# Storing turned pairs in 512-byte runs and loading each back in one transfer of 4 KB runs

## Chip, cores and metric

The kernel runs on one core of one Trainium2 chip. The metric is device time in microseconds, the median over runs of one execution each. Engines are named as in the profile: PE (TensorE), DVE (VectorE), ACT (ScalarE), POOL (GpSimd) and SP (SyncE, which issues every transfer of this kernel on one queue).

## What is computed

A gated layer over `x` of 64 sequences x 128 tokens x 512 features, float32: a cross-attention branch whose score matrix is summed over the batch, and a feed-forward branch, each added to `x` through a tanh gate.

```python
# attention branch on LN(x), context c
Q, K, V = LN(x) @ Wh, c @ Wh, c @ Wh          # per head, 4 heads of 128
A = max(|sum_b(Q K^T / sqrt(hd)) * decay|, 1)
O = A V
Y = (O - mean(O)) / sqrt(var(O) + 1e-3) * gamma + beta
x1 = x + tanh(g1) * ((relu(LN(x) @ Wg) * Y) @ Wo)
# feed-forward branch
x2 = LN(x1)
out = x1 + tanh(g2) * (silu(x2 @ Gate * gs) * (x2 @ Up * us)) @ Down * ds
```

## The kernel before

The 64 sequences are 64 tiles `t` of 128 tokens. The kernel runs in three stages. The first (to about 345 us) makes V, W and the score sum group by group of four sequences. The second, `first_groups`, runs 8 groups of 15 steps: 11 steps multiply 512 tokens of x2 with the gate and up weights (`up_mm`), 4 steps multiply the hidden tiles with the down weights (`down_mm`). Between these steps, the attention branch of pairs of tiles `q` is carried on in 13 pieces, a new pair every 3.5 steps (`pieces`, `first_step`). The third stage takes the other 32 tiles in 4 passes of 8, with products of sums and differences of weights (`seven`, `down_of`).

TensorE wants Y and x2 turned, features on the partitions, and in float32 split into a high and a low part. From the third pair on it doesn't turn them itself. The path is:

- DVE transposes each tile of 128 tokens x 512 features in blocks of 32 x 32 (`y_blocks` into `tbuf`, L1006; `x2_blocks` into `xbuf`, L1053). This turns inside each group of 32 partitions.
- SyncE stores the pair to DRAM (`y_out`, L377, to `wy_scratch`; `x2_out`, L381, to `x2_scratch`), 4 KB from each partition.
- SyncE loads it back with the blocks where they belong: `blocks_in` (L421 to L426) issues four transfers, one for each 32 partitions of the destination, in runs of 128 bytes. `y_in` fills `turned[0]`, `x2_in` fills `turned[1]` for the second stage, and `pair_in` fills `fa` and `fb` for the third.
- ACT applies gamma and beta to Y (`y_pair_affine`, L666) in place, DVE multiplies with W (`wy_pair_mul`, L1017), ACT and POOL split the product (`wy_pair_hi`, L706; `wy_pair_lo`), and PE multiplies it with Wo (`wo_pair`). For x2, ACT copies the high part (`x2_pair_hi`, L711) and DVE makes the low one (`x2_pair_lo`, L1057); in the third stage `operand_hi` (L729), `operand_lo` and `combine` prepare seven operands from `fa` and `fb`.

Every engine runs its own list in program order, and waits on semaphores at its head. So what sets the order around the change is: on SyncE, in pair `q`'s pieces, `y_out` (piece 3), `y_in` (4; it waits for the store and for the multiply of the pair before), `w_load` (5), `x_again` (6), `x2_out` and `x1_store` (12), and `x2_in` at steps 9 and 12 of a group; on ACT, `x2_pair_hi` at steps 11 and 13, ahead of that step's pieces; on DVE, `x2_pair_lo` in the same steps, ahead of the transposes, the multiply and x1 of these steps, and ahead of the next `finish` (L1167), which frees the bank that PE's next product needs.

Of the kernel before, what the change touches and what calls it, by code (L numbers as in the profile page):

```python
# [9 lines left out]
NS = 8  # L10
# [65 lines left out]
def gated_layer(nc, x, ctx_t, wh, wh_t, wg, wo, gate_t, up_t, down_t, cols, rows, decay, eye, out):  # L76
# [6 lines left out]
    with stack:  # L83
# [26 lines left out]
        stg = misc[:, 512:1216]  # L110
        tbuf = misc[:, 0:1024].rearrange("p (t n) -> p t n", t=2)
# [4 lines left out]
        xbuf = placed("xbuf", [128, 2, 512])  # L116
        a_parts = [a[:, :].rearrange("p (h n) -> p h n", h=4) for a in a_sb]
# [54 lines left out]
        oper = [[over(f"op{i}{part}", *units[2 * i + part], [128, 2, 512], f32r) for part in range(2)] for i in range(7)]  # L172
        fa = over("fa", "reg", 44, [128, 2, 4, 256])
        fb = over("fb", "reg", 60, [128, 2, 4, 256])
        hall = over("hall", "reg", 0, [128, NI, 1024])
# [47 lines left out]
        bank_p6 = pz  # L223

        def before_split(o):

            a1, a2, b1, b2 = fa[:, :, 0:2, :], fa[:, :, 2:4, :], fb[:, :, 0:2, :], fb[:, :, 2:4, :]
            return {A1: a1, T1: a1, A2: a2, T4: a2, T3: b1, B2: b2, T2: b2}[o]

        def split(o, i):  # L230

            return oper[o][i][:, :, :].rearrange("p k (h n) -> p h k n", h=2)

# [37 lines left out]
        def wt_of(q):  # L271

            return xbuf[:, :, :].rearrange("p t (k n) -> p (t k) n", n=256) if q == 1 else raw[:, 2:4, :].rearrange("p t (k n) -> p (t k) n", n=256)

# [15 lines left out]
        def _(e):  # L290
# [81 lines left out]
            def y_out(q):  # L372

                p.wait_ge("wyb", 2 * q - 2)
                if q > 2:
                    p.wait_ge("wyl", 64 * (q - 2))
                e.dma_start(wy_s.rearrange("t p n -> p t n"), tbuf).then_inc(s["wys"], 16)  # L377
# [33 lines left out]
            def pair_in(q):  # L411

                p.wait_ge("x2s", 16 * (q - 1))
# [5 lines left out]
                blocks_in(x2_s[q], to[:, q % 2, :, :], "x2l")  # L419

            def blocks_in(scratch, dst, name):  # L421

                src = scratch.rearrange("t (u r) (c a j) -> a r c (t u) j", u=4, c=4, a=4)
                for a in range(4):
                    to = dst[32 * a:32 * a + 32, :, :].rearrange("r c (x j) -> r c x j", j=32)
                    e.dma_start(to, src[a]).then_inc(s[name], 16)  # L426

            def y_in(q):
                p.wait_ge("wys", 16 * (q - 1))
                p.wait_ge(*(("wm", q + 2) if q > 2 else ("wm", 4)))  # L430
                blocks_in(wy_s, turned[0], "wyl")

            def x2_in(q):
                p.wait_ge("x2s", 16 * (q - 1))
                if q > 2:
                    p.wait_ge("tb2e", q + 2)
                blocks_in(x2_s[q], turned[1], "x2l")

# [162 lines left out]
        def _(e):  # L601
# [61 lines left out]
            def affine(dst, src):  # L663

                for k in range(4):
                    last = e.activation(dst[:, k, :], src[:, k, :], ACT.Identity, bias=colsb[:, 2 * NI + 6 + k:2 * NI + 7 + k],  # L666
                                        scale=colsb[:, 2 * NI + 2 + k:2 * NI + 3 + k])
                last.then_inc(s["aff"])
# [8 lines left out]
            def y_pair_affine(q):  # L677
                p.wait_ge("wyl", 64 * (q - 1))
                affine(turned[0], turned[0])

# [27 lines left out]
            def x2_pair_hi(q):  # L708
                p.wait_ge("x2l", 64 * (q - 1))
                p.wait_ge("um", 11 * (q // 2))  # L710
                e.copy(x2_pair(q, 0), turned[1][:, :, :]).then_inc(s["tb2h"])  # L711

# [6 lines left out]
            def operand_hi(m, k):  # L719
                o = (A1, B2, A2, T1, T2, T3, T4)[k]  # L720
                if k == 0 and m == 0:
                    p.wait_ge("um", NI * NS)
                elif k == 0:
                    p.wait_ge("p4", NI * m)
                if k == 0:
                    p.wait_ge("x2l", 64 * (2 * NS + 4 * m + 2))
# [30 lines left out]
            def split_hi(m, part):  # L757
# [5 lines left out]
                else:  # L763
                    p.wait_ge("wo", B)
                    p.wait_ge("wylo", B // 2 - 2)
                    p.wait_ge("tb2e", 2 + 2 * NS)
                    p.wait_ge("x2s", 16 * (B // 2 - 2))
                e.copy(hsp[t % 2][0][:, i0:i1, :], hall[:, i0:i1, 128 * i:128 * i + 128]).then_inc(s["hsh"])  # L768
# [144 lines left out]
        def _(e):  # L913
# [85 lines left out]
            def y_blocks(t):  # L999
                p.wait_ge("nr", t + 1)  # L1000
                if t >= 6:
                    p.wait_ge("wys", 16 * (t // 2 - 2))
                else:
                    p.wait_ge("alo", 1)
                    p.wait_ge("wolo", 4)
                e.transpose(tbuf[:, t % 2, :], nbuf[:, t % 2, :]).then_inc(s["wyb"])  # L1006

# [41 lines left out]
            def x2_blocks(t):  # L1049
                p.wait_ge("xn2", t + 1)  # L1050
                if t >= 6:
                    p.wait_ge("x2s", 16 * (t // 2 - 2))
                e.transpose(xbuf[:, t % 2, :], xn[:, t % 2, :]).then_inc(s["x2b"])  # L1053

            def x2_pair_lo(q):
                p.wait_ge("tb2h", q + 3)
                e.tensor_tensor(x2_pair(q, 1), turned[1][:, :, :], f(x2_pair(q, 0)), ALU.subtract).then_inc(s["tb2e"])  # L1057

            def combine(m, k):

                a1, a2, b1, b2 = fa[:, :, 0:2, :], fa[:, :, 2:4, :], fb[:, :, 0:2, :], fb[:, :, 2:4, :]
                dst, x, y = ((a1, b1, a1), (b1, b2, b1), (b2, b2, a1), (a2, a2, b2))[k]
# [3 lines left out]
                p.wait_ge("opt", 4 * m + k)  # L1066
                p.wait_ge("x2l", 64 * (2 * NS + 4 * m + 2))
                e.tensor_tensor(dst, x, y, ALU.subtract).then_inc(s["opt"])
# [862 lines left out]
```

## Time and profile before

| | |
|---|---|
| median of 3 runs | 1529.16 us (1528.46 to 1529.73) |
| the profiled execution | 1533.71 us |
| its span, first to last instruction | 1531.7 us |
| mean granted TensorE clock | 0.996 |
| busy PE, DVE, ACT, POOL | 98%, 69%, 45%, 47% |
| DMA packets | 374598, of which 258336 under 512 B |

In the profile a line such as L1017 is the line of kernel.py that issued the instruction. `out<-in` names the tiles, "SPq" is an issue on SyncE's queue, and a wait or idle time is followed by what ended it. A chain is the work that ended last, followed back step by step. "PEclk" is the TensorE clock that was granted as a share of full speed. The DMA share is the mean busy share of the core's 16 DMA engines.

### The profile page before, as it was taken

The page shows a single profiled execution, that of the slowest core. Times are in us where ns is not written, and L with a number is a line of the kernel's source. Part 1 is how long each engine was busy: PE and PEld are TensorE (multiplying, and loading weights), DVE is VectorE, ACT ScalarE, POOL GpSimd, SP SyncE. Part 2 cuts the span into 40 slices and gives each one's busy share as a digit, 9 for nine tenths or more (in the row PEclk, how much of TensorE's full clock was granted, in tenths as well). Part 3 has the DMA queues.
Part 4 walks back from the last instruction along what each step waited for, and adds up shares of the span by engine and source line. Part 5 has one row for each costly group of instructions (what it writes and reads, how often), then busy time and mean ns, then how long its engine had stood idle before and what let it go on. Part 6 is the DMA issues. An engine that isn't in the chain of part 4 may idle for free.

```text
span 1531.7 us, 20329 instructions
## 1 busy us (share of the span) xinstructions
PE 1500.3 (98%) x7226; PEld 1259.3 (82%) x7226; DVE 1058.3 (69%) x1497; ACT 684.0 (45%) x1067; POOL 723.4 (47%) x775
## 2 busy tenths in 40 slices
PE   6999999999899999999999999999999999999998
PEld 5888888887788888888887888888788888888887
DVE  6677778785557676577765777563767777778772
ACT  3444434445454545455353554534344444343442
POOL 4556666762353544445352544524227338237236
PEclk9999999999999999999999999999999999999999
DMA  6888888866678687787776777686273473472422
GB/s 227 270 266 267 262 281 286 265 216 205 199 220 219 200 213 222 210 252 221 220 228 181 211 219 216 182 239 170 89 214 127 114 213 104 142 209 94 132 102 83
DMA packets 374598, 305.93 MB, mean 200 GB/s; under 512 B 258336, under 2 KB 284320, under 8 KB 374304
## 3 DMA queue, kind: packets, MB, share of 16 engines
q1 hardware_dynamic: 374496, 304.61, 66.6%
q8 instruction: 59, 0.97, 0.2%
q14 instruction: 43, 0.35, 0.1%
HBM read 200.23 MB, written 117.31 MB: 207 GB/s over the span
## 4 chain that ended last, share of the span: by engine, by line
PE 83%; DVE 5%; DMA 4%; POOL 3%; ACT 2%; issue 2%; SPq 2%; DVEq 0%; ACTq 0%; POOLq 0%
PE ps L1670 37%; PE pyb L1554 8%; PE po L1670 8%; PE ptb L1670 5%; PE pyb L1670 5%; PE ps L1589 5%; PE po L1554 4%; PE pyb L1654 3%; PE ptb L1654 3%; PE ptb L1658 2%; PE pyb L1658 2%; SPq L426 1%; PE ptb L1559 1%; DMA wy_scratch<-misc 1%; POOL reg L1432 1%
## 5 line engine op out<-in xcount | busy, mean ns | idle before, releaser
L1385 POOL TENSOR_SCALAR rs<-mv 128x1 f32<-128x1 f32 (+1 forms) x132 | 53.1, 402 | 296.7 <-DVE mv L1034 141.3
L1670 PE MATMUL ps<-reg,gate 128*128 128x512 f32 x704 | 177.6, 395 | 4.4 <-DVE tmp L1167 2.6
L1473 POOL TENSOR_TENSOR reg<-tmp,reg 128x512 fp32r<-128x512 f32 x88 | 118.0, 1342 | 131.2 <-ACT reg L717 131.2
L1554 PE MATMUL pyb<-reg,xreg 128*128 128x512 f32 x720 | 178.6, 396 | 0.8 <-DVE xreg L947 0.8
L1670 PE MATMUL ps<-reg,up 128*128 128x512 f32 x704 | 174.4, 390 | 0.0
L1670 PE MATMUL ps<-op,wbuf 128*128 128x512 f32 x704 | 173.9, 389 | 0.0
L1670 PE MATMUL ps<-xreg,reg 128*128 128x512 f32 x704 | 163.4, 390 | 1.3 <-DVE tmp L1167 1.3
L1457 POOL TENSOR_TENSOR p5b<-p5b,p1b 128x512 f32<-128x512 f32 x44 | 57.0, 1295 | 218.1 <-ACT p5b L741 218.1
L1670 PEld LDWEIGHTS ps<-reg,gate 128*128 128x128 f32 x704 | 132.2, 190 | 31.9 <-issue 3.0
L1670 PEld LDWEIGHTS ps<-reg,up 128*128 128x128 f32 x704 | 132.8, 189 | 27.8
L1670 PEld LDWEIGHTS ps<-xreg,reg 128*128 128x128 f32 x704 | 131.5, 188 | 29.1 <-DVE tmp L1167 1.8
L1670 PEld LDWEIGHTS ps<-op,wbuf 128*128 128x128 f32 x704 | 132.1, 188 | 27.4
L1554 PEld LDWEIGHTS pyb<-reg,xreg 128*128 128x128 f32 x720 | 131.8, 188 | 27.6 <-DVE xreg L947 1.5
L1468 POOL TENSOR_TENSOR hsp<-hall,hsp 128x640 fp32r<-128x640 f32 (+2 forms) x72 | 136.6, 1914 | 34.6 <-ACT hsp L768 33.5
L1670 PE MATMUL po<-op,wbuf 128*128 128x512 f32 x528 | 134.6, 389 | 0.0
L1160 DVE SCALAR_TENSOR_TENSOR tmp<-ps,colsb,tmp 128x512 f32<-128x512 f32 x88 | 65.5, 744 | 87.5 <-PE ps L1670 83.3
L1436 POOL TENSOR_TENSOR wyt<-raw,wyt 128x1024 fp32r<-128x1024 f32 x30 | 75.1, 2504 | 90.8 <-ACT wyt L706 90.8
L1670 PEld LDWEIGHTS po<-op,wbuf 128*128 128x128 f32 x528 | 99.1, 188 | 20.6
L778 ACT ACTIVATE tmp<-ps,colsb 128x512 f32<-128x512 f32 x88 | 60.6, 688 | 121.3 <-PE ps L1670 108.7
L1589 PE MATMUL ps<-reg 128*128 128x256 f32 x768 | 101.1, 284 | 1.5 <-DVE misc L953 1.1
L1589 PEld LDWEIGHTS ps<-reg 128*128 128x128 f32 x768 | 96.9, 191 | 5.4 <-ACT tmp L626 1.5
L1388 POOL TENSOR_TENSOR rs<-rs,nhalf 128x1 f32<-128x1 f32 (+1 forms) x132 | 88.8, 672 | 11.0
(153 smaller groups left out, 2829.5 us busy)
## 6 DMA issues: line engine op xcount, KB each, us to landing
wbuf<-ws_scratch SPq DMA_DIRECT2D x44, 896.0 KB, 4.9
xr<-in_x SPq DMA_DIRECT2D x63, 512.0 KB, 5.7
raw<-in_ctx_t SPq DMA_DIRECT2D x32, 512.0 KB, 4.7
w_scratch<-tmp SPq DMA_DIRECT2D x64, 256.0 KB, 5.0
v_scratch<-tmp SPq DMA_DIRECT2D x64, 256.0 KB, 4.2
raw<-v_scratch SPq DMA_DIRECT2D x32, 512.0 KB, 6.1
x_scratch<-xr SPq DMA_DIRECT2D x32, 512.0 KB, 4.6
xr<-x_scratch SPq DMA_DIRECT2D x32, 512.0 KB, 6.0
```

Source lines behind the costliest of these rows:

```text
L778: e.activation(tmp[:, m % 3, :], banks[2 * (n % 2)], ACT.Silu, scale=colsb[:, j:j + 1]).then_inc(s["si"])
L1160: e.scalar_tensor_tensor(tmp[:, m % 3, :], banks[2 * (n % 2) + 1], colsb[:, NI + j:NI + j + 1], tmp[:, m % 3, :], ALU.mult, ALU.mult).then ...
L1388: e.tensor_tensor(dst, dst, nhalf[:, 0:dst.shape[-1]], ALU.pow).then_inc(s[name])
L1436: e.tensor_tensor(wyt[1][:, :, :], wt_of(q), f(wyt[0][:, :, :]), ALU.subtract).then_inc(s["wylo"])
L1457: e.tensor_tensor(p5b[n % 2][:, :], p5b[n % 2][:, :], p1b[n % 2][:, :], ALU.add).then_inc(s["p15"])
L1468: e.tensor_tensor(hsp[t % 2][1][:, i0:i1, :], hall[:, i0:i1, 128 * i:128 * i + 128], f(hsp[t % 2][0][:, i0:i1, :]), ALU.subtract).then_inc ...
L1473: e.tensor_tensor(hid[1][:, m % 11, :], tmp[:, m % 3, :], f(hid[0][:, m % 11, :]), ALU.subtract).then_inc(s["hlo"])
L1554: last = e.matmul(dst, lhs[a], rhs[b], start=(k == 0 and i == 0), stop=(k == n - 1 and i == 2))
L1589: last = e.matmul(ps[t % 2][:, h, :, :], ct[g % 2][i][:, h, 128 * b:128 * b + 128], wh_and_z(q, h, b), start=(n == 0), stop=(n == 2))
L1654: e.matmul(py(t), wyt_of(t)[0][:, k, :], wos[i][k], start=(k == 0 and i == 0), stop=False)
L1658: last = e.matmul(py(t), wyt_of(t)[1][:, k, :], wos[0][k], start=False, stop=(k == 3))
L1670: last = e.matmul(dst, l, r, start=(k == 0 and i == 0), stop=(k == n - 1 and i == 1), skip_group_check=sums)
```

## The change

The two scratch tensors get the shape [j 32, (a t) 8, u 4, 128], so that what one destination partition needs lies together in 4 KB. DVE's transposes write their blocks in another order (`blocks_to`, `blocks_of`), so that each partition holds eight runs of 128 elements (512 bytes). A pair is stored in four transfers, one for each 32 partitions `u`, in runs of 512 bytes (`blocks_out`). It is loaded in one transfer to 128 partitions, 4 KB each, whose source is walked as 4 `a`, 32 `j`, 4 KB. The tokens and features now lie in each loaded partition as 8 groups (32 tokens each) of 4 runs (feature blocks) of 32 elements, and the instructions that read it (L666, L711, L1017, L1057, `operand_hi`, `operand_lo`, `combine`) walk it in these runs (`by_part`, `tokens_by_32`, `half_of`). The number of compute instructions and their element counts stay. A load counts 16 on its semaphore instead of 64, a store 64 instead of 16.

```diff
-        wy_s = nc.dram_tensor("wy_scratch", [2, 128, D], f32, kind="Internal").ap()
-        x2_s = nc.dram_tensor("x2_scratch", [B // 2, 2, 128, D], f32, kind="Internal").ap()
+        wy_s = nc.dram_tensor("wy_scratch", [32, 8, 4, 128], f32, kind="Internal").ap()
+        x2_s = nc.dram_tensor("x2_scratch", [B // 2, 32, 8, 4, 128], f32, kind="Internal").ap()
...
+        def half_of(pairs, i):
+
+            return pairs[:, :, :].rearrange("p q (x d n) -> p (q x) d n", x=8, d=2)[:, :, i, :]
...
+        def by_part(pair):
+
+            return pair.rearrange("p (x c r) -> p c x r", x=8, c=4)
+
+        def tokens_by_32(pair):
+            return pair.rearrange("p c (x r) -> p c x r", x=8)
+
+        def blocks_to(pair, t):
+
+            return pair.rearrange("p (a t c r) -> p t a c r", a=4, t=2, c=4)[:, t % 2, :, :, :]
+
+        def blocks_of(tile):
+
+            return tile.rearrange("p (c a j) -> p a c j", c=4, a=4)
...
             def x2_out(q):
                 p.wait_ge("x2b", 2 * q - 2)
-                e.dma_start(x2_s[q].rearrange("t p n -> p t n"), xbuf[:, :, :]).then_inc(s["x2s"], 16)
+                blocks_out(x2_s[q], xbuf[:, :], "x2s")
...
+            def blocks_out(scratch, pair, name):
+
+                for u in range(4):
+                    e.dma_start(scratch[:, :, u, :], pair[32 * u:32 * u + 32, :].rearrange("j (x n) -> j x n", x=8)).then_inc(s[name], 16)
...
             def blocks_in(scratch, dst, name):
 
-                src = scratch.rearrange("t (u r) (c a j) -> a r c (t u) j", u=4, c=4, a=4)
-                for a in range(4):
-                    to = dst[32 * a:32 * a + 32, :, :].rearrange("r c (x j) -> r c x j", j=32)
-                    e.dma_start(to, src[a]).then_inc(s[name], 16)
+                e.dma_start(dst, scratch.rearrange("j (a t) u n -> a j (t u n)", a=4)).then_inc(s[name], 16)
...
-                e.tensor_tensor(wt_of(q), wt_of(q), turned[0][:, :, :], ALU.mult).then_inc(s["wm"])
+                wt = tokens_by_32(wt_of(q))
+                e.tensor_tensor(wt, wt, by_part(flat(turned[0])), ALU.mult).then_inc(s["wm"])
...
-                e.transpose(xbuf[:, t % 2, :], xn[:, t % 2, :]).then_inc(s["x2b"])
+                e.transpose(blocks_to(xbuf[:, :], t), blocks_of(xn[:, t % 2, :])).then_inc(s["x2b"])
```

## Rows read from the trace of the kernel before

**Rows 1.** The page: span, and part 1 (busy us, share, instructions).

```profile
span 1531.7 us, 20329 instructions
...
PE 1500.3 (98%) x7226; PEld 1259.3 (82%) x7226; DVE 1058.3 (69%) x1497; ACT 684.0 (45%) x1067; POOL 723.4 (47%) x775
```

**Rows 2.** TensorE's waits, 380 to 1110 us: total, times, longest us.

```profile
PE ps L1670 <- DVE tmp L1167: 3.9, 2, 2.6
...
PE pyb L1654 <- ACT wyt L706: 1.0, 1, 1.0
...
PE ps L1670 <- DVE tmp L1160: 0.4, 1, 0.4
```

**Rows 3.** Windows: length, busy PE, PEld, DVE, ACT, POOL, clock, DMA share, GB/s.

```profile
406.00:408.00 2.00, 2.00 (x10) 1.68 (x9) 0.00 (x0) 1.65 (x3) 1.19 (x2) 1.00 1.06 411
...
552.72:635.17 82.45, 82.45 (x388) 69.19 (x387) 56.55 (x83) 43.81 (x66) 38.99 (x47) 1.00 0.79 217
...
840.00:850.00 10.00, 9.04 (x33) 7.31 (x34) 9.59 (x15) 4.76 (x7) 7.31 (x9) 0.83 0.36 110
...
1044.00:1046.00 2.00, 2.00 (x10) 1.65 (x10) 0.33 (x1) 1.88 (x3) 0.82 (x1) 1.00 1.08 172
```

**Rows 4.** SyncE's queue, timelines 396:480 and 800:845: start, us.

```profile
437.19 3.55 SPq L426 DMA_DIRECT2D turned<-wy_scratch  x4
...
817.71 4.06 SPq L426 DMA_DIRECT2D turned<-wy_scratch  x4
...
821.81 0.67 SPq L381 DMA_DIRECT2D x_scratch<-xbuf  x1
...
823.98 6.55 SPq L426 DMA_DIRECT2D turned<-x_scratch  x4
```

**Rows 5.** Chain that ended last, 795 to 860 us: start, us.

```profile
821.81 3.37 DMA x_scratch<-xbuf
...
833.55 1.06 ACT reg L711
```

**Rows 6.** Chain that ended last, 390 to 480 us.

```profile
443.97 6.18 DMA x_scratch<-xr
...
458.70 1.06 ACT reg L711
```

**Rows 7.** Lines L426, L381: issue in ns, least, median, most.

```profile
L426 SPq DMA_DIRECT2D turned<-wy_scratch x120: 557/668/3211, 411.8 to 1008.5; - x120
...
L381 SPq DMA_DIRECT2D x_scratch<-xbuf x30: 360/665/1113, 443.6 to 1052.8; - x30
```

**Rows 8.** The page's part 6: KB each, median us to landing.

```profile
out<-xr SPq DMA_DIRECT2D x31, 512.0 KB, 2.8
```

**Rows 9.** Timelines of DVE, ACT and PE at two chains' ends.

```profile
478.17 1.23 DVE L1057 TENSOR_TENSOR reg<-turned,reg 128x1024 fp32r<-128x1024 f32 x1 [1.18 <-ACT reg L711]
...
481.49 2.00 PE L1670 MATMUL ps<-reg,gate 128*128 128x512 f32 x8
...
923.57 1.05 ACT L711 CAST reg<-turned 128x1024 fp32r<-128x1024 f32 x1 [6.09 <-DMA turned<-x_scratch]
...
927.04 1.05 ACT L706 CAST wyt<-raw 128x1024 fp32r<-128x1024 f32 x1 [2.42 <-DVE raw L1017]
...
930.41 1.98 PE L1654 MATMUL pyb<-reg,wyt 128*128 128x512 f32 x8
```

**Rows 10.** Lines L1006, L1017, L666: duration in ns, least, median, most.

```profile
L1006 DVE STREAM_TRANSPOSE misc<-nbuf x60: 659/711/714, 398.6 to 999.2; 128x512 f32<-128x512 f32 x60
...
L1017 DVE TENSOR_TENSOR raw<-raw,turned x30: 1179/1226/2298, 421.2 to 1028.6; 128x1024 f32<-128x1024 f32 x30
...
L666 ACT ACTIVATE turned<-turned,colsb x120: 586/588/604, 418.2 to 1025.9; 128x256 f32<-128x256 f32 x120
```

**Rows 11.** ScalarE's waits, whole span: total, times, longest us.

```profile
ACT reg L711 <- DMA turned<-x_scratch: 45.8, 9, 8.2
```

**Rows 12.** Timeline of ScalarE, 1055 to 1096 us.

```profile
1068.74 1.05 ACT L729 CAST op<-fa 128x1024 fp32r<-128x1024 f32 x1
```

More of the change, by code:

```diff
@@ L110, in gated_layer @@
         stg = misc[:, 512:1216]
-        tbuf = misc[:, 0:1024].rearrange("p (t n) -> p t n", t=2)
+        tbuf = misc[:, 0:1024]
         wyt = [placed(f"wyt{i}", [128, 4, 256], f32r) for i in range(2)]
@@ L115, in gated_layer @@
         a_sb = [placed(f"a{i}", [128, 512], f32r) for i in range(2)]
-        xbuf = placed("xbuf", [128, 2, 512])
+        xbuf = placed("xbuf", [128, 1024])
         a_parts = [a[:, :].rearrange("p (h n) -> p h n", h=4) for a in a_sb]
@@ L172, in gated_layer @@
         oper = [[over(f"op{i}{part}", *units[2 * i + part], [128, 2, 512], f32r) for part in range(2)] for i in range(7)]
-        fa = over("fa", "reg", 44, [128, 2, 4, 256])
-        fb = over("fb", "reg", 60, [128, 2, 4, 256])
+        fa = over("fa", "reg", 44, [128, 2, 1024])
+        fb = over("fb", "reg", 60, [128, 2, 1024])
         hall = over("hall", "reg", 0, [128, NI, 1024])
@@ L223, in gated_layer, with flat @@
         bank_p6 = pz
+        def half_of(pairs, i):
+            return pairs[:, :, :].rearrange("p q (x d n) -> p (q x) d n", x=8, d=2)[:, :, i, :]
         def before_split(o):
-            a1, a2, b1, b2 = fa[:, :, 0:2, :], fa[:, :, 2:4, :], fb[:, :, 0:2, :], fb[:, :, 2:4, :]
-            return {A1: a1, T1: a1, A2: a2, T4: a2, T3: b1, B2: b2, T2: b2}[o]
+            a1, a2, b1, b2 = half_of(fa, 0), half_of(fa, 1), half_of(fb, 0), half_of(fb, 1)
+            return {A1: a1, T1: a1, A2: a2, T4: a2, T3: b1, B2: b2, T2: b2}[o].rearrange("p x (k r) -> p x k r", k=2)
         def split(o, i):
-            return oper[o][i][:, :, :].rearrange("p k (h n) -> p h k n", h=2)
+            return oper[o][i][:, :, :].rearrange("p k (x r) -> p x k r", x=16)
+        def flat(pair):
+            return pair[:, :, :].rearrange("p c n -> p (c n)")
+        def by_part(pair):
[6 more added lines that the diff above has]
+            return tile.rearrange("p (c a j) -> p a c j", c=4, a=4)
         def down_bank(t):
@@ L271, in wt_of @@
         def wt_of(q):
-            return xbuf[:, :, :].rearrange("p t (k n) -> p (t k) n", n=256) if q == 1 else raw[:, 2:4, :].rearrange("p t (k n) -> p (t k) n", n=256)
+            return xbuf[:, :].rearrange("p (k n) -> p k n", k=4) if q == 1 else raw[:, 2:4, :].rearrange("p t (k n) -> p (t k) n", n=256)
         def tile_of(pair, t):
@@ L375, in y_out @@
                 if q > 2:
-                    p.wait_ge("wyl", 64 * (q - 2))
-                e.dma_start(wy_s.rearrange("t p n -> p t n"), tbuf).then_inc(s["wys"], 16)
+                    p.wait_ge("wyl", 16 * (q - 2))
+                blocks_out(wy_s, tbuf, "wys")
             def x2_out(q):
                 p.wait_ge("x2b", 2 * q - 2)
-                e.dma_start(x2_s[q].rearrange("t p n -> p t n"), xbuf[:, :, :]).then_inc(s["x2s"], 16)
+                blocks_out(x2_s[q], xbuf[:, :], "x2s")
             def sums_store(u):
@@ L411, in pair_in @@
             def pair_in(q):
-                p.wait_ge("x2s", 16 * (q - 1))
+                p.wait_ge("x2s", 64 * (q - 1))
                 if q < 2 * NS + 4:
@@ L665, in affine @@
                 for k in range(4):
-                    last = e.activation(dst[:, k, :], src[:, k, :], ACT.Identity, bias=colsb[:, 2 * NI + 6 + k:2 * NI + 7 + k],
+                    last = e.activation(dst[:, k], src[:, k], ACT.Identity, bias=colsb[:, 2 * NI + 6 + k:2 * NI + 7 + k],
                                         scale=colsb[:, 2 * NI + 2 + k:2 * NI + 3 + k])
@@ L677, in y_pair_affine @@
             def y_pair_affine(q):
-                p.wait_ge("wyl", 64 * (q - 1))
-                affine(turned[0], turned[0])
+                p.wait_ge("wyl", 16 * (q - 1))
+                affine(by_part(flat(turned[0])), by_part(flat(turned[0])))
             def wy_hi(t):
@@ L708, in x2_pair_hi @@
             def x2_pair_hi(q):
-                p.wait_ge("x2l", 64 * (q - 1))
+                p.wait_ge("x2l", 16 * (q - 1))
                 p.wait_ge("um", 11 * (q // 2))
-                e.copy(x2_pair(q, 0), turned[1][:, :, :]).then_inc(s["tb2h"])
+                e.copy(tokens_by_32(x2_pair(q, 0)), by_part(flat(turned[1]))).then_inc(s["tb2h"])
             def hidden_hi(m):
@@ L725, in operand_hi @@
                 if k == 0:
-                    p.wait_ge("x2l", 64 * (2 * NS + 4 * m + 2))
+                    p.wait_ge("x2l", 16 * (2 * NS + 4 * m + 2))
                 if k >= 3:
@@ L766, in split_hi @@
                     p.wait_ge("tb2e", 2 + 2 * NS)
-                    p.wait_ge("x2s", 16 * (B // 2 - 2))
+                    p.wait_ge("x2s", 64 * (B // 2 - 2))
                 e.copy(hsp[t % 2][0][:, i0:i1, :], hall[:, i0:i1, 128 * i:128 * i + 128]).then_inc(s["hsh"])
@@ L1001, in y_blocks @@
                 if t >= 6:
-                    p.wait_ge("wys", 16 * (t // 2 - 2))
+                    p.wait_ge("wys", 64 * (t // 2 - 2))
                 else:
@@ L1005, in y_blocks @@
                     p.wait_ge("wolo", 4)
-                e.transpose(tbuf[:, t % 2, :], nbuf[:, t % 2, :]).then_inc(s["wyb"])
+                e.transpose(blocks_to(tbuf, t), blocks_of(nbuf[:, t % 2, :])).then_inc(s["wyb"])
             def wy_mul(t):
@@ L1066, in combine @@
                 p.wait_ge("opt", 4 * m + k)
-                p.wait_ge("x2l", 64 * (2 * NS + 4 * m + 2))
+                p.wait_ge("x2l", 16 * (2 * NS + 4 * m + 2))
                 e.tensor_tensor(dst, x, y, ALU.subtract).then_inc(s["opt"])
```

16 lines of the change are left out of this document (8 added, 8 removed).

## The prediction

> **What bounds the kernel now.** I read the page first: TensorE (PE) is busy 1500.3 of 1531.7 us [rows 1], so a transfer can move the end only where PE stands still. Next come PE's waits: from 380 to 1110 us, where the changed code runs, it waits 3.9 us for `finish` (L1167), 1.0 us for the W*Y halves (L706) and 0.4 us for the hidden tile (L1160) [rows 2]; the waits on L1042 and L1047 there end before the first changed transfer. The windows give the price of one such stop: PE idled 2.6 us at 838 to 841 and the granted clock in 840 to 850 was then 0.83, so 1.7 us went with it; over whole groups without a stop PE is busy 82.45 of 82.45 us at clock 1.00 [rows 2, 3]. So the ceiling on any gain is 2.6 + 1.7 + 1.0 + 0.4 = 5.7 us. The 1.3 us left of the 3.9 (later) come from the operand preparation on VectorE, whose loads are long in, and I leave them.
>
> **The stop at 838 us.** The queue's timeline and the chain of waits show it: SyncE's four parts of the Y load take 4.06 us to issue, only then go out the x2 store, the x1 store and the W load; the x2 store lands 3.37 us after issue, and the four parts of the x2 load, issued from 823.98 to 830.53 us with a wait inside, land at 833.55 [rows 4, 5]. ScalarE stands in `x2_pair_hi` (L711) until then, VectorE behind it in `x2_pair_lo`, and queued behind that are two transposes, two residual adds with their statistics and the `finish` that frees PE's bank. PE is 2.6 us late. The same chain at 451 to 464 us costs 1.0 us (L711, transposes, L1017, L706) [rows 6].
>
> **What the queues can carry.** A plain load in long runs moved 411 GB/s at a DMA share near 1; loads in 128-byte runs moved 172 GB/s at the same share [rows 3]. So the 524,288 bytes of a pair take 3.1 us now, on all 16 engines, and would take 1.3 us in 4 KB runs on 16. One engine alone then carries about 411/16 = 25.7 GB/s.
>
> **Part 1, the store.** One transfer becomes four of 32 partitions. For the issue the nearest rows are L426, also 32 partitions each (median 0.67, least 0.557 us), against 0.36 to 0.67 for the single store [rows 7]: about 2.4 us for four instead of 0.5, so +1.9 us of SyncE per pair, and the last quarter leaves 1.8 us later. It applies 30 times to Y and 30 times to x2; behind it on SyncE stand the x1 store, the W load and the next x load. In data: 128-byte runs cost 3.1 us for 256 runs on each engine, 12.1 ns a run, of which 5 ns is the bytes; with the same 7 ns over, 64 runs of 512 B cost 64 x (20 + 7) = 1.7 us, against 1.3. Bounds 1.3 and 3.1; I take 1.7.
>
> **Part 2, the load.** Four issues become one: SyncE gets back 3 x 0.67 = 2.0 us at the median and up to 4.06 - 0.6 = 3.5 in the stopped chain. It pays for part 1. The data is the open point. The new source is walked as 4 blocks `a`, then 32 rows `j`, then 4 KB. Every other transfer that I find in the kernel has a first walk of 128, 32 or 352. If the hardware deals a transfer out by its first walk, this one goes to 4 engines, not 16: 131,072 B on each, 5.1 us, where the others get nothing. No row of before decides it. The Trainium skill ("DMA: Bandwidth & Descriptors", sections on why a DMA increments its semaphore by 16 and on rules for kernel authors) says just this: the number of engines is the largest up to 16 that divides the slowest dimension of both sides, so 4 here. That rule speaks against the change, and no run here shows it yet.
>
> With 4 engines, the stopped chain goes so (a fixed 1.5 us from issue to first data: the 512 KB store of the output at the median lands in 2.8 us [rows 8], less 1.3). The Y load is issued at 817.7, and fills the four until 817.7 + 1.5 + 5.1 = 824.3. The x2 quarters wait behind it and end at 826.0 (825.2 before). The x2 load is issued at 826.1; x1 store and W load are ahead of it, 1.3 us each, to 828.6; it lands at 833.7, or 0.5 to 1 us later if part of the 1.5 us comes at the end: +0.2 to +1.2 against 833.55. I take +0.9. The chain at 451: the Y load issued at 437.2 [rows 4] ends at 443.8, W load, x2 and x1 stores behind it by 448.1 to 448.6 (before, the x1 store landed at 450.15 [rows 6]), so x again and V load start 1.6 us sooner and the x2 load, 5.1 instead of 3.1 us and 0.6 less in issue, lands within 1 us of 458.70. I take 0.
>
> **Where there is slack.** In the other groups the distance from the end of the chain to the PE instruction that needs it is: `x2_pair_lo` ends at 479.40, the gate product starts at 481.49, 2.1 us; L706 ends at 928.1, PE's `wo_pair` starts at 930.41, 2.3 us [rows 9]. I found no shorter one in the rest. A shift of 0.9 is hidden there. Over a group of 82.45 us the DMA share is 0.79, 65 us, of which 6.3 pair loads of 3.1 are 19.5 [rows 3]; the four engines would then hold 45.5 + 8.6 x 0.4 + 6.3 x 5.1 = 81 us of 82.45, the others far less. Shares over 1 occur [rows 3], so these seconds overlap in part and the true load is lower. That is the danger of this change.
>
> **Part 3, engine work.** DVE's transposes, ScalarE's copies and affines and the multiplies keep their element counts and now walk runs of 32 elements. The transposes (711 ns), L1017 (1226 ns) and L666 (588 ns) [rows 10] cost the same per element whether their runs are 128, 256 or 512 long elsewhere in the kernel; runs of 32 aren't in the trace. Bounds: 0 and double. I take 0, since a transpose already works in blocks of 32 and costs 711 ns. What hides a small excess is VectorE's 69% [rows 1], except in the two chains above. Operand preparation after 1068 us uses the same walks; ScalarE takes its first operand at 1068.74 [rows 12], and four loads of 5.1 us from 1038 on are in by 1061.
>
> **Sum, likeliest case (A).** Stall +0.9, clock in the measured proportion 1.7/2.6 x 0.9 = 0.6: +1.5 us on the profiled execution's 1533.71, 1535.2. That execution ran 4.55 us above the median 1529.16 of the runs shown; I carry the difference over: 1530.7.
>
> **Rivals.**
> B, faster: the load spreads over 16 engines. In the stopped chain Y data end at 820.5, the x2 stores land by 823, and the x2 load lands near 827 instead of 833.5; both stops vanish with their clock loss, -5.7: 1523.5. For it: the whole backlog of L426 goes. Against: the first walk of 4. It decides at the number of engines; with 8 the load takes 2.6 us, less than now, and the change would gain.
> C, slower: four engines and no overlap. Each of two loads in a chain brings its excess of 2.0, the quarters 1.8, SyncE gives back 3.5: about +2.5 everywhere. Stops: +2.5, +2.5, and 0.4 + 0.2 where the slack is 2.1 and 2.3, clock 0.65 x (2.5 + 3.5) = 3.9: +9.5, 1538.7. It decides once the shift passes the 2.1 us of slack.
> D, faster: four engines, but SyncE's freed time counts for more. In the chain at 913 us W, x and V loads are queued ahead; the x2 load would land near 922 against 923.57 [rows 9]. If -1.5 held at the two stops: -1.5 - 1.7 - 1.0 = -4.2, 1525.0.
> E, slower: runs of 32 cost half as much again on VectorE. L1057 and two transposes in one chain, with L1017 in the other: +1.2 and +1.9, clock 2: about +5, 1534.
>
> **How the numbers follow.** Chances: A 0.42, B 0.22, C 0.24, D 0.06, E 0.06. A measurement of this kernel tells about 0.2% (3 us) from no change, so "same" is 1526.1 to 1532.2. Faster: 0.21 of B, 0.04 of D, 0.25. Same: 0.32 of A, 0.06 of the others, 0.38. Slower: 0.10 of A, 0.23 of C, 0.04 of E, 0.37. A's own range is 1527 to 1535. The range reaches down to B and up past C: 1523 to 1541.
>
> **What would show it.** Landing of the single load: 6.5 us and more from issue with A and C, near 3 with B. DMA share in 1038 to 1053 us: with A about a quarter of the engines busy for 20 us; with B all busy for some 5. ScalarE's idle time ahead of L711 (45.8 us in 9 waits before [rows 11]): about the same with A, near zero with B, over 60 with C. L1006, L1017 and L666 at 711, 1226 and 588 ns, or E. PE's wait for L1167: 3.9 + 0.9 with A, 1.3 with B. What would make it wrong: PE stops at places where none is now, above all `wo_pair` and the first gate product of a group; or a queue that lets later transfers pass the long load.

## The result and the profile after

The changed kernel takes 1602.16 us (median; 1598.0 to 1605.5), the one before 1529.45 us (1528.46 to 1530.47) beside it: 1.0469 times as long, 95% interval 1.0456 to 1.0483, 73 us slower where 1.5 us were forecast. The profiled execution has a span of 1595.9 us at a mean granted clock of 0.984. In the text below lines are those of the changed kernel: `blocks_in` is L452, `blocks_out` L448, `x2_pair_hi` L737, the affine L692, `wy_pair_hi` L732, `finish` L1194, the x1 store L381, `x_again` L377. Each kernel of an experiment has line numbers of its own.

The page of the kernel after, its head and the line on packets (before: [rows 1] and the table):

```profile
span 1595.9 us, 20329 instructions
...
PE 1516.4 (95%) x7226; PEld 1267.6 (79%) x7226; DVE 1055.7 (66%) x1497; ACT 683.5 (43%) x1067; POOL 712.5 (45%) x775
...
DMA packets 181878, 305.93 MB, mean 192 GB/s; under 512 B 11856, under 2 KB 99280, under 8 KB 181584
```

The small packets are gone, as they should be, the busy times of DVE and ACT are what they were, and PE stands still for 80 us instead of 31. TensorE's waits from 380 to 1110 us say where (total, times, longest us; the rows of before that bear on the change are [rows 2], 5.3 us):

```profile
PE pyb L1681 <- ACT wyt L732: 20.2, 5, 7.7
PE ps L1697 <- DVE tmp L1194: 18.7, 3, 9.8
PE po L1581 <- DVE reg L1010: 4.8, 1, 4.8
PE pyb L1681 <- DVE xr L1055: 4.7, 1, 4.7
PE ps L1697 <- DVE reg L1084: 2.9, 1, 2.9
```

PE now stops ahead of `wo_pair` (L1681) for 24.9 us and of the first gate product (L1084 makes its low half) for 2.9 us, where it waited 1.0 us and nothing, and its wait for `finish` is 18.7 us instead of 3.9. These are engines that were late; what made them late stands one step back, in ScalarE's waits for transfers over the whole span (before: 45.8 us in 9 [rows 11]):

```profile
ACT reg L737 <- DMA turned<-x_scratch: 115.0, 14, 16.8
ACT turned L692 <- DMA turned<-wy_scratch: 26.3, 8, 10.6
```

The windows of the kernel after (columns as in [rows 3]): the second stage from 440 us to the issue of the first load for the third stage; a stretch just behind a stop; and a stretch in which only the loads for the third stage (`pair_in`) run:

```profile
440.00:1102.21 662.21, 612.36 (x2764) 507.91 (x2764) 406.68 (x594) 294.93 (x444) 264.00 (x327) 0.96 0.65 195
...
478.00:481.00 3.00, 3.00 (x9) 2.35 (x8) 2.97 (x4) 0.00 (x0) 2.92 (x3) 0.50 0.74 230
...
1104.00:1108.00 4.00, 4.00 (x19) 3.32 (x18) 1.26 (x3) 1.68 (x3) 2.00 (x5) 1.00 0.24 84
```

The last row points to the cause. The share of busy DMA engines is 0.24, about 4 of 16, at 84 GB/s, where the same loads in 128-byte runs had 1.08 and 172 GB/s [rows 3]. The first row is the bill: the stage has 49.9 us of idle PE. The second is the rest of it: after PE's 5.99 us stop the granted clock was 0.50, 1.2 of 2.4 GHz.

One stop followed back, in SyncE's queue and then in the chain that ended last (start, us, what):

```profile
477.98 0.57 SPq L452 DMA_DIRECT2D turned<-wy_scratch  x1
479.34 0.56 SPq L368 DMA_DIRECT2D raw<-w_scratch  x1
481.02 0.32 SPq L354 DMA_DIRECT2D raw<-v_scratch  x1
481.44 0.55 SPq L452 DMA_DIRECT2D turned<-x_scratch  x1
```

```profile
453.66 6.18 DMA x_scratch<-xr
459.86 0.39 SPq L377
...
460.80 10.33 DMA turned<-x_scratch
...
481.44 15.56 DMA turned<-x_scratch
...
497.02 1.05 ACT reg L737
...
498.10 1.24 DVE reg L1084
```

The load of x2 issued at 460.80 lands 10.33 us later, the one at 481.44 15.56 us later: a load of Y is on the same four engines 3.5 us ahead of it, with W and V between. Ten loads of x2 stand in the chain between 440 and 1110 us, 8.36 to 15.56 us each. PE's timeline shows the same two as stops, in brackets the idle time:

```profile
476.91 3.78 PE L1681 MATMUL pyb<-reg,wyt 128*128 128x512 f32 x8 [5.99 <-ACT wyt L732]
...
499.38 1.22 PE L1697 MATMUL ps<-reg,gate 128*128 128x512 f32 x2 [2.88 <-DVE reg L1084]
```

And the transfers that use all engines come late too: the x1 store's median landing is 8.4 us (4.6 before, 4.4 in the kernel with sixteen engines, below), and SyncE stands in `x_again` until an x1 store has landed, with the V and x2 loads behind it. In the chain from 440 to 1110 us these stores (`x_scratch<-xr`) take as much as the x2 loads, 16 of them with 121 us in all:

```profile
by line: DMA turned<-x_scratch 18.2%; DMA x_scratch<-xr 18.1%; PE ps L1697 14.1%; SPq L448 8.8%; issue 5.6%; DMA raw<-v_scratch 5.5%; DMA wy_scratch<-misc 3.6%; DVE xbuf L1080 2.5%; PE pyb L1681 1.9%; PE ptb L1681 1.9%; DVE raw L1044 1.7%; 
```

### The profile page after: what moved, and what is told of

The parts are those of the page before. It is cut to its first block, busy times and chain, and to the rows that moved or that the text cites. A ratio compares the mean times of both kernels' runs of the same rounds, so it can differ in the third digit from the quotient of the medians.

```text
span 1595.9 us, 20329 instructions
## 1 busy us (share of the span) xinstructions
PE 1516.4 (95%) x7226; PEld 1267.6 (79%) x7226; DVE 1055.7 (66%) x1497; ACT 683.5 (43%) x1067; POOL 712.5 (45%) x775
## 4 chain that ended last, share of the span: by engine, by line
PE 53%; DMA 23%; DVE 8%; SPq 5%; issue 3%; POOL 3%; ACT 3%; ACTq 0%; DVEq 0%; POOLq 0%
PE ps L1697 18%; DMA turned<-x_scratch 8%; DMA x_scratch<-xr 8%; PE po L1697 8%; PE pyb L1581 7%; PE ptb L1697 5%; PE pyb L1697 5%; PE ps L1616 5%; SPq L448 4%; DMA raw<-v_scratch 3%; PE po L1581 2%; DMA wy_scratch<-misc 2%; DMA turned<-wy_scratch 1%; PE ptb L1586 1%; DVE xbuf L1080 1%
## 5 line engine op out<-in xcount | busy, mean ns | idle before, releaser
L1697 PE MATMUL ps<-reg,gate 128*128 128x512 f32 x704 | 181.1, 401 | 18.4 <-DVE tmp L1194 13.2
L1412 POOL TENSOR_SCALAR rs<-mv 128x1 f32<-128x1 f32 (+1 forms) x132 | 49.9, 378 | 312.9 <-DVE mv L1061 158.3
L1084 DVE TENSOR_TENSOR reg<-turned,reg 128x1024 fp32r<-128x1024 f32 x14 | 17.2, 1225 | 124.5 <-ACT reg L737 124.5
```

What stands on the lines that cost most here:

```text
L1084: e.tensor_tensor(tokens_by_32(x2_pair(q, 1)), by_part(flat(turned[1])), f(tokens_by_32(x2_pair(q, 0))), ALU.subtract).then_inc(s["tb2e"])
L1412: e.tensor_scalar(dst, var, eps, None, ALU.add).then_inc(s["eps"])
L1697: last = e.matmul(dst, l, r, start=(k == 0 and i == 0), stop=(k == n - 1 and i == 1), skip_group_check=sums)
```

## Experiments

Theory 1: the single load runs on four DMA engines, and that alone makes the loss. Rivals: the stores in four parts of 512-byte runs; the engines' walks in runs of 32 elements; the order of the issues. First, everything kept except the number of engines.

**Sixteen engines.** The scratch is laid out so that one load walks 128 partitions first, in two runs of 2 KB; stores still in four parts and 512-byte runs, compute still in runs of 32. The walks of the stores and transposes follow the new layout.

```diff
-        wy_s = nc.dram_tensor("wy_scratch", [32, 8, 4, 128], ...)
+        wy_s = nc.dram_tensor("wy_scratch", [8, 32, 4, 128], ...)
...
-                e.dma_start(dst, scratch.rearrange("j (a t) u n -> a j (t u n)", a=4)).then_inc(s[name], 16)
+                e.dma_start(dst.rearrange("p (t n) -> p t n", t=2),
+                            scratch.rearrange("(t a) j u n -> (a j) t (u n)", t=2)).then_inc(s[name], 16)
```

> Scratch laid out as 8 groups (t a), 32 rows j, then 2 KB, so that the one load walks 128 partitions first (2 runs of 2 KB each); the four-part stores in 512-byte runs and all engine work stay as in the changed kernel. Theory 1 (the single load goes to 4 of the 16 DMA engines, and that costs all 72 us): the load lands about 3 us after issue, ScalarE's wait ahead of x2_pair_hi falls under 45 us, median 1522 to 1530. Rival (the four-part stores or the reads in runs of 32 cost the time): stays above 1580.

Measured: 1526.79 us, 0.9969 of before [0.9958, 0.9980]. In this kernel TensorE's wait for `finish`, ScalarE's for x2, the window of the second stage, and the landing of the x1 store (KB each, median us):

```profile
PE ps L1699 <- DVE tmp L1196: 1.3, 1, 1.3
```

```profile
ACT reg L739 <- DMA turned<-x_scratch: 22.4, 6, 5.7
```

```profile
440.00:1032.93 592.93, 592.93 (x2761) 496.55 (x2760) 400.87 (x582) 287.66 (x434) 264.18 (x319) 1.00 0.69 216
```

```profile
x_scratch<-xr SPq DMA_DIRECT2D x32, 512.0 KB, 4.4
```

PE is busy 592.93 of 592.93 us and no transfer is left in this stage's chain. The loads land in 3.9 us (Y) and 5.9 us (x2) at the median, where about 3 were expected. The whole loss is gone and a gain of 0.3% is in its place: neither the stores nor the walks in runs of 32 cost anything that reaches the end. The same stage is 69.3 us shorter than in the kernel after (662.21); of these, 49.9 are idle PE and 19.4 are nearly the same products (2764 and 2761) at a lower clock (612.36 - 592.93).

**Four loads.** The layout of the change to the byte, but the load issued as four transfers of 32 partitions.

```diff
-                e.dma_start(dst, scratch.rearrange("j (a t) u n -> a j (t u n)", a=4)).then_inc(s[name], 16)
+                src = scratch.rearrange("j (a t) u n -> a j (t u n)", a=4)
+                for a in range(4):
+                    e.dma_start(dst[32 * a:32 * a + 32, :], src[a]).then_inc(s[name], 16)
```

> The changed kernel with its layout and stores, but the load split into four transfers, one for each 32 partitions, 4 KB runs. Theory 1: each part is walked as 32 rows first and uses 16 engines, so 1524 to 1533, a little behind the sixteen-engine single load because of three more issues per pair. Rival (stores or run length of the reads): above 1580.

Measured: 1530.47 us, 0.9996 [0.9986, 1.0006]. The same bytes from the same places, in the same 4 KB runs: only the outer walk is taken apart, and the loss is gone. That is the closest test of theory 1, and it holds. Against the kernel with one load it is 0.3% behind, and ScalarE's wait for x2 is 33.1 us instead of 22.4; three more issues a load and the length of the runs both differ, and which of them it is was not parted.

**Stores and loads exchanged.** One store in 2 KB runs, four loads in 512-byte runs, all over sixteen engines.

```diff
-                for u in range(4):
...
+                e.dma_start(scratch.rearrange("t u j a n -> (u j) t (a n)"), pair.rearrange("p (t n) -> p t n", t=2)).then_inc(s[name], 16)
...
+                for a in range(4):
+                    e.dma_start(dst[32 * a:32 * a + 32, :].rearrange("j (x n) -> j x n", n=128),
+                                scratch[:, :, :, a, :].rearrange("t u j n -> j (t u) n")).then_inc(s[name], 16)
```

> The other way to split the work: one store of a pair (128 partitions, 2 KB runs) and four loads of 32 partitions in runs of 512 bytes, all walked as 128 or 32 first. Read against the sixteen-engine single load. If the landing of the x2 chain is what is left to win, one store issue saves 1.8 us ahead of the load and four load issues cost 1.8 us after it: 1524 to 1530, the same within 0.2%. If the short runs or SyncE's issues matter more than thought: 1531 to 1537.

Measured: 1527.04 us, 0.9974 [0.9963, 0.9984], the same as with sixteen engines and stores in four. Whether the four parts and the 512-byte runs are on the store's side or on the load's makes no difference that can be seen.

**One half of the change at a time.** The sixteen-engine kernel, with only the load of Y, or only those of x2, walked as four blocks.

```diff
+                if name == "x2l":
+                    e.dma_start(dst.rearrange("p (t n) -> p t n", t=2),
+                                scratch.rearrange("(t a) j u n -> (a j) t (u n)", t=2)).then_inc(s[name], 16)
+                else:
+                    e.dma_start(dst, scratch.rearrange("j (a t) u n -> a j (t u n)", a=4)).then_inc(s[name], 16)
```

> Only the Y load keeps the walk of 4 blocks; the x2 loads of both stages walk 128 partitions first. Theory 1a (the four engines have more work than time in the mean): 45.5 + 3.4 + 4.3 x 5.6 + 2 x 1.4 = 76 us of work in a group of 82.45, so no loss, 1525 to 1533. Theory 1b (what counts is the burst at a group's end, where Y load and x2 load follow each other): the x2 load still waits about 4 us behind the Y load, 1532 to 1550.

> Only the x2 loads keep the walk of 4 blocks; the Y load walks 128 partitions first. Theory 1a: 45.5 + 3.4 + 4.3 x 1.4 + 2 x 5.6 = 66 us of work in 82.45, no loss, 1525 to 1533. Theory 1b: the x2 load alone takes 4.2 us longer on its four engines, with nothing in front of it: 1530 to 1545; both halves together then make less than the 72 us, because the waits add up only when both are there.

Measured: Y alone 1546.15 us, 1.0097 [1.0073, 1.0120]; x2 alone 1539.32 us, 1.0051 [1.0031, 1.0070]. Over the sixteen-engine kernel these are +1.28% and +0.82%, together 2.1%; both at once cost 5.0%. The losses don't add: more than half is there only when both loads are on the four engines. ScalarE's wait for x2 rises even where only Y is moved (the first fence: Y alone; the second: x2 alone; 22.4 us with neither), so Y's load delays another load that is itself spread over sixteen (the profiled execution with x2 alone is the slowest of its seven, 1547.83 us, so its 70.3 is at the high end):

```profile
ACT reg L744 <- DMA turned<-x_scratch: 49.2, 10, 11.3
```

```profile
ACT reg L744 <- DMA turned<-x_scratch: 70.3, 11, 13.6
```

Theory 1a, that the four engines cost nothing as long as they have time to spare in the mean, said 1525 to 1533 for both and fails both, for Y clearly: 76 of 82.45 us were expected there, and it still costs 1.3%. Both results lie in the ranges of 1b, in which bursts count. The median landings of the x1 store, spread over sixteen engines in both kernels (first Y alone, then x2 alone), show a second way in which Y's load does harm:

```profile
x_scratch<-xr SPq DMA_DIRECT2D x32, 512.0 KB, 8.4
```

```profile
x_scratch<-xr SPq DMA_DIRECT2D x32, 512.0 KB, 4.3
```

**A load that nobody waits for.** To part the load's own landing from what it does to others: the sixteen-engine kernel with one more 512 KB copy from DRAM to DRAM behind each x1 store, awaited only at the end of the kernel, walked as 4 blocks (shown) or as 128 rows (`src[0:128, :]` into `spare[q]`).

```diff
+            def extra(q):
+                src = x.rearrange("b s d -> (b s d)").rearrange("(k n) -> k n", n=1024)
+                src = src.rearrange("(a j) n -> a j n", j=64)[0:4, 0:32, :]
+                e.dma_start(spare[q].rearrange("(a j) n -> a j n", a=4), src).then_inc(s["extra"], 16)
```

> The sixteen-engine kernel plus, for each pair, one copy of 512 KB from x to a spare DRAM buffer, issued behind the x1 store, walked as 4 blocks first; no engine ever waits for it before the end (extra work, nothing left out). Theory 1a/1b (four engines short of time, later transfers stand behind): these four get 30 x 6 = 180 us more work in the 610 us of the second stage, 427 + 180 = 607, so about full: 1540 to 1575. Rival (only the chain store, load, copy counts, not the engines' load): 1524 to 1531, as without it.

> The same extra copy of 512 KB per pair, walked as 128 rows first. Theory 1a/1b: 30 x 1.6 = 48 us on each engine, 475 of 610 us, all engines with time to spare: 1525 to 1532. Rival (any 512 KB more in the queue costs, however spread, because of the issue or the memory): as with the walk of 4.

Measured: on four engines 1547.37 us, 1.0105 [1.0089, 1.0120]; on sixteen 1526.98 us, 0.9968 [0.9956, 0.9980]. As many bytes more cost nothing when spread and 20.4 us when not, though nothing waits for them. The landings of V and W, both spread over all engines, on four (first fence) and on sixteen (second), show how:

```profile
raw<-v_scratch SPq DMA_DIRECT2D x32, 512.0 KB, 9.4
...
raw<-w_scratch SPq DMA_DIRECT2D x31, 512.0 KB, 10.1
```

```profile
raw<-v_scratch SPq DMA_DIRECT2D x32, 512.0 KB, 6.9
...
raw<-w_scratch SPq DMA_DIRECT2D x31, 512.0 KB, 6.8
```

That fits a spread transfer being in only when the slowest of its sixteen engines is, with four of them behind the long copy. It is inferred: the views name no engines.

**The transfers by themselves.** A kernel of SyncE alone, which computes nothing of the layer (all of that is left out): transfers of 512 KB, each issued when the one before has landed.

> Nothing of the reference is computed: SyncE alone moves 512 KB per transfer, each waited for before the next, three turns. Loads of 128 partitions whose source is walked as 128 rows, as 4 blocks, as 8, as 2 (all in 4 KB runs), one in 128-byte runs; a store in 4 KB runs and one in four parts in 512-byte runs; a load walked as 4 blocks with a plain load right behind it. If the first walk sets the number of engines: about 3.0, 7, 4.3 and 12 us from issue to landing, 4.8 in 128-byte runs, stores 3.0 and 5.0, and the pair 8.4. If all go over 16 engines: about 3.0 for each of the four walks. The time of the whole program says nothing of the kernel.

In the second of three turns the loads start at (walk of 128, 4, 8 and 2 blocks; then, after 87.90, the load in 128-byte runs, the store in 4 KB runs, the store in four parts of 512-byte runs, and a walk of 4 with a plain load right behind it):

```profile
56.72 0.33 SPq L30 DMA_DIRECT2D walk<-in_x  x1
...
59.97 0.62 SPq L30 DMA_DIRECT2D walk<-in_x  x1
...
68.43 0.60 SPq L30 DMA_DIRECT2D walk<-in_x  x1
...
75.28 0.52 SPq L30 DMA_DIRECT2D walk<-in_x  x1
...
87.90 0.59 SPq L30 DMA_DIRECT2D runs<-in_x  x1
92.33 0.33 SPq L30 DMA_DIRECT2D whole_d<-walk  x1
94.96 2.59 SPq L30 DMA_DIRECT2D quarters_d<-walk  x4
99.34 0.59 SPq L30 DMA_DIRECT2D long<-in_x  x1
99.98 0.47 SPq L30 DMA_DIRECT2D behind<-in_x  x1
109.42 0.34 SPq L30 DMA_DIRECT2D out<-behind  x1
```

From start to start: 128 rows 3.25 us, 4 blocks 8.46, 8 blocks 6.85, 2 blocks 12.62, 128-byte runs 4.43, one store 2.63, four-part store 4.38. The other two turns give 3.3 and 3.5, 8.7 and 8.9, 6.5 and 6.6, 12.6 and 12.7, 4.5, 2.6 and 4.4 in this order. In the turn shown the walks of 4 and 8 blocks and the pair take 1.5 to 2.6 us longer than was expected; the others are within 0.7. The windows inside them (length, busy POOL, clock, DMA share, GB/s): walks of 4, of 2 and of 8:

```profile
64.00:66.00 2.00, 0.00 (x0) 1.00 0.26 98
...
80.00:84.00 4.00, 0.00 (x0) 1.00 0.13 53
...
70.00:74.00 4.00, 0.00 (x0) 1.00 0.44 120
```

Shares of 0.26 and 0.13 are 4 and 2 of 16 engines, at 24 to 27 GB/s each; 0.44 is 7, nearly 8, at only 15 GB/s each. The number of engines follows the first walk. The Trainium skill ("DMA: Bandwidth & Descriptors", on why a DMA increments its semaphore by 16) states the rule as the largest number up to 16 that divides the slowest dimension of both sides, and adds that on a hardware queue these are the lowest-numbered engines. The shares agree with the first half; no view here names the engines, and the second half is not shown, though the delays of one load of four by another fit it. A plain load right behind the walk of 4 is in 10.08 us after the first issue (10.5 and 11.7 in the other turns), 1.6 us later than the walk of 4 by itself: it too waits for those four.

**Is it the bytes, or the number?** The kernel after, with each load of Y bringing half its columns.

```diff
+                if name == "wyl":
+                    e.dma_start(dst[:, 0:512], scratch.rearrange("j (a t) u n -> t a j (u n)", a=4)[0]).then_inc(s[name], 16)
```

> The kernel after, with one thing less: each load of turned Y brings only the first half of its columns (2 KB of the 4 KB of every partition), still walked as four blocks; the second half of turned Y isn't loaded, so that part of the computation is left out. Waits, stores and the load of x2 are those of the kernel after. Over the second stage four of the 16 DMA engines have, by the shares of its trace, some 362 us of other work and 44 loads of 6.1 us each, together 630 of 670 us. The theory that the loss comes from those four engines being nearly full for the whole stage: 30 loads lose about half of 6.1 us, 92 us in all, the four fall to about 540 us of a stage of some 615, and most of the loss goes, not half: 1535 to 1560 us, near the 1539.3 us of the kernel in which x2 alone is walked as four blocks. The rival, that each load costs in proportion to its bytes, by its own landing: halfway between the kernel after (1602.2) and the one with x2 alone on four blocks (1539.3), about 1571 us, with 1563 to 1580 counted for it. The rival that the number of four-block loads matters and not their bytes: 1590 us or more.

Measured: 1547.65 us, 1.0102 [1.0080, 1.0123]. Of the 5.0% over the sixteen-engine kernel 3.7 go with half of one load's bytes. It lies in the range of the theory that the four engines are nearly full, and outside both rivals: the loss is far from linear in the bytes, and it isn't set by the number of loads. The arithmetic in the expectation (44 loads, 630 of 670 us) was looser than it looked, since the two stretches it compared didn't hold quite the same work; it is done again, as an estimate, below.

**Less beside them.** The opposite cut: the loads whole, V, W and output reduced to 16 of 128 partitions (the output's store isn't shown); with the same cut on sixteen engines as control.

```diff
+                n = 16 if q > 4 else 128
+                e.dma_start(raw[0:n, 0:2, :], v_s[0:n, 2 * q:2 * q + 2, :]).then_inc(s["vld"], 16)
...
+                e.dma_start(wt_of(q)[0:n, :, :], w_s[q // 2, 0:n, :, 256 * (q % 2):256 * (q % 2) + 256]).then_inc(s[f"wl{q % 2}"], 16)
```

> The kernel after with less traffic beside the loads on four engines: from the sixth pair on, the loads of V and of W bring only 16 of 128 partitions, and the output of the first 32 tiles is stored for 16 partitions only. The rest of V, W and the output is left out, so that part of the computation is too; every issue, wait and semaphore stays where it is. About 69 transfers of 512 KB shrink to 64 KB in the second stage; at 1.3 us of each engine for 512 KB that is 78 us less on every engine, of a stage of some 662 us. The theory that the loss comes from those four engines having too much to do, others' traffic and loads together: the stage falls most of the way back, 1535 to 1570 us. The rival that a load on four engines costs through its own longer landing (8.46 us alone against 3.25) in the chains that wait for it, whatever else is moved: 1590 us or more.

> Control for the run with less traffic beside the loads: the same cut (V, W and output of 16 partitions; the rest of them is left out of the computation) in the kernel whose pair loads use sixteen engines. TensorE is busy there for the whole second stage (592.93 of 592.93 us), so by every theory less traffic brings nothing: 1524 to 1528 us, as the 1526.8 us without the cut.

Measured: 1568.70 us, 1.0264 [1.0235, 1.0292]; control 1526.66 us, 0.9971 [0.9960, 0.9982]. The control is where it should be. The run itself is at the very end of the first range and below the second: taking other transfers' work off those engines takes back 2.1 of the 5.0%, and 2.9% stay although the DMA share is down to 0.53. TensorE's waits, and the chain where it passes two loads of x2 in this kernel:

```profile
PE ps L1700 <- DVE tmp L1197: 11.0, 3, 6.7
PE pyb L1684 <- ACT wyt L735: 9.3, 4, 5.7
```

```profile
455.20 9.50 DMA turned<-x_scratch
...
475.05 13.51 DMA turned<-x_scratch
```

So neither theory has it alone. Even in this quieter queue the eight loads of x2 that stand in the second stage's chain take 9.21 to 14.60 us from issue to landing, and the x1 store, which was not reduced, 8.0 us at the median. The x1 stores, the loads of x and the stores of pairs still use the four engines too, so what would be left without any other traffic isn't shown.

**How full are the four?** With sixteen engines the second stage of 592.93 us has a DMA share of 0.69 (first window of that kernel), 409 us on each engine. The 42 pair loads of the stage (28 of Y, 14 of x2) make 55 us at the 1.3 us of the prediction; 354 is other work (277 with the cut, by the control's share of 0.56). A load on four engines takes 5.1 us of each (the prediction's) to 6.5 us (8.46 alone, less the 1.95 that are not data when spread, 3.25 - 1.3). The busy shares of the loads alone agree: over the three walks of 4 they come to 5.8 to 6.2 us of each of the four (0.17 of 8.46 us, times 4, in the turn shown), though a spread load comes to 1.7 us and not 1.3 (0.52 of 3.25). An estimate for each of the four, against the 593 us that the stage takes unstopped:

| kernel (half a load counted as half) | us of each of the four | share of 593 | x1 store, median landing | over its sixteen-engine partner |
|---|---|---|---|---|
| after | 354 + 42 x 5.1 to 6.5 = 568 to 627 | 96 to 106% | 8.4 us | +5.0% |
| extra copy on four | 409 + 29 x 5.1 to 6.5 = 557 to 598 | 94 to 101% | 4.6 us | +1.4% (nobody waits for it) |
| Y on four | 372 + 28 x 5.1 to 6.5 = 515 to 554 | 87 to 93% | 8.4 us | +1.3% |
| less beside | 277 + 42 x 5.1 to 6.5 = 491 to 550 | 83 to 93% | 8.0 us | +2.9% |
| half of Y | 354 + 28 x 5.1 to 6.5 = 497 to 536 | 84 to 90% | 5.0 us | +1.3% |
| x2 on four | 390 + 14 x 5.1 to 6.5 = 461 to 481 | 78 to 81% | 4.3 us | +0.8% |

Fullness alone doesn't give the loss. The extra copy fills the four almost as far as the kernel after and costs 1.4%, not 5.0, and there nobody waits for it; and the fourth row costs twice as much as rows that are as full. The two rows with the largest loss are those in which Y and x2 are both whole on the four engines: there the awaited x2 loads are late, and the x1 store is late too (8.0 and 8.4 us, as with Y alone, against 4.3 to 5.0 in the other three). So the runs show that work on those four engines costs even when it isn't awaited, and that awaited loads there cost most together. That the four are nearly full is an estimate, and how fullness, the x2 loads and the x1 stores share the 73 us stays open.

## Why the prediction was wrong

**What bounds the kernel, and the ceiling.** Right. The ceiling of 5.7 us, made of the stops that [rows 2] show and their clock, is what the sixteen-engine kernel all but reaches: its span is 1526.2 against 1531.7 us, its ratio 0.9969. Its wait for `finish` is 1.3 us, the part I had left out as not the change's.

**Part 1, the store.** Right in size. The four issues take 2.5 to 3.0 us at 43 of 60 places where 2.4 was taken (up to 8.7 at the others), and at the end the kernel with four-part stores and one load is no slower than the one with a single store and four loads (0.9969 and 0.9974). Alone they land in 4.38 us against 2.63, 1.75 us later, near the 1.8 of the text. That the x1 store stands behind them was said, but not that it would come to stand in the chain.

**Part 2, number of engines.** The question was the right one and four the right answer; the likeliest case, C and D had it, B did not.

**Part 2, the size.** Wrong, the first of two steps that failed. The landing was put at 1.5 + 5.1 = 6.6 us; the walk of 4 takes 8.46 us alone, and the loads of x2 in the chain 8.36 to 15.56. The rate of one engine was right (25.7 GB/s said, 24.5 measured); the 1.5 us around it was too little. The excess over a spread load is 5.2 us (8.46 - 3.25), not 5.1 - 1.3 = 3.8. And the sum let only one load's excess into the chain, +0.9, because SyncE's freed issue time was set against it; in the chain at 477.98 to 497.02 stand the x1 store, the Y load, W, V and the x2 load, and if all need the same four, an estimate is 1.5 + 2 x 6.5 + 3 x 1.3 = 18.4 us, measured 19.0 (477.98 to 497.00).

**"The true load is lower".** Wrong, and the larger step. The text worked out 81 of 82.45 us of work for each of the four engines in every group and then set it aside, because shares over 1 occur. The estimate above, 96 to 106%, repeats that number, and the text named it as the danger and then gave it no term in the sum. What the runs showed in its place is late transfers in every group, those spread over sixteen engines included: ten x2 loads and sixteen x1 stores stand in the stage's chain, where the text had two stops and one load. The 2.1 or 2.3 us of slack [rows 9] behind which a shift was to hide are less than the 4.0 us by which such a load, alone, lands later than one in 128-byte runs (8.46 - 4.43), and the waits come at `wo_pair`, at `finish` and at the first gate product; the first and the last of these the last paragraph had named as what would make it wrong. The extra copy limits this reading: four engines nearly as full cost 1.4% when nobody waits for the long transfer.

**Clock.** The measured proportion was taken from one stop, 1.7 us for 2.6 (0.65). Over the stage it is 19.4 us for 49.9, 0.39. The direction was right, the size not what decided.

**Part 3 and E.** Right, and E falls: the runs of 32 elements cost nothing. The same instructions after, in ns least, median and most (before: [rows 10], 711, 1226 and 588):

```profile
L1032 DVE STREAM_TRANSPOSE misc<-nbuf x60: 661/708/716, 397.3 to 1063.4; 128x512 f32<-128x512 f32 x60
```

```profile
L1044 DVE TENSOR_TENSOR raw<-raw,turned x30: 1181/1226/2298, 423.5 to 1092.4; 128x1024 f32<-128x1024 f32 x30
```

```profile
L692 ACT ACTIVATE turned<-turned,colsb x120: 583/588/605, 420.9 to 1089.7; 128x256 f32<-128x256 f32 x120
```

**Rivals and range.** C, four engines without overlap, was the nearest mechanism, at +2.5 us for each shift and 1538.7 us in all. It was priced at two stops, not as a delay in every group, and it had no price for the x1 stores. The range ended at 1541, since no case was worked out in which the queue on four engines hardly empties. B's price, 1523.5, was nearly right (the sixteen-engine kernel is 4.7 us under before by its ratio, 5.7 were said), and it is about what the change would have given with another outer walk. B's remark that eight engines would still gain (2.6 us a load) isn't borne out: the walk of 8 took 6.85 us alone, longer than the 4.43 of 128-byte runs over sixteen. No kernel with eight was run.

## What to carry to other kernels

Look at the outermost walk of a transfer before its run length: here 4 KB runs walked as 4 blocks were worth less than 128-byte runs walked over all engines, and the same bytes in four transfers of 32 rows, or in one of 128 rows with 2 KB runs, took the loss away. When a change concentrates work on part of a resource, compute the occupancy of that part over the whole stage, and if it comes out near the time that the stage takes, price it as a queue that doesn't empty, and look for what stands behind it in program order: here a slack of 2 us was not enough, and stores that the change hadn't touched took as much of the chain as the x2 loads. A transfer that nobody waits for still costs, when it holds engines that every other transfer needs.

## What the runs showed of the hardware that was not expected

- A walk of 8 blocks was to take 4.3 us and took 6.85, at 120 GB/s with a share of 0.44: eight engines carried 15 GB/s each, where four carried 24.5 (98 GB/s) and two 26.5 (53 GB/s). Why is open; one run shows it, in three turns, and its walks differ also in how far apart the blocks lie in DRAM (512, 256 and 128 KB for 2, 4 and 8 blocks).
- One 512 KB copy on four engines, awaited by nothing, raised the median landing of V from 6.9 to 9.4 us and of W from 6.8 to 10.1, over the same copy spread over sixteen.
- A 512 KB load in 128-byte runs is in after 4.43 us when nothing else runs, 1.2 us behind one in 4 KB runs (3.25) and far ahead of the one on four engines (8.46): here short runs were much the cheaper of the two.
